# Three shared input buffers, a reordered batch and no closing drain of GpSimd in a gated cross-attention kernel with routed experts

## The chip, the cores and the metric

The kernel runs on one core of a Trainium2 chip. The metric is the device time of one execution in microseconds, lower is better. Engines are named as in the profile: PE (TensorE matmul), PEld (TensorE weight load), DVE (VectorE), ACT (ScalarE), POOL (GpSimd) and SP (SyncE, which here only issues DMAs).

## The reference

x and ctx are (8, 512, 512) float32: 8 batches of 512 rows of width 512. The first layer is a two-way cross-attention between the row-normalised x and ctx, mixed by a gate; the second is a mixture of 8 experts with one expert for each row.

```python
x = x + tanh(g_xattn[0]) * xattn(layernorm(x), ctx)       # see below
x = x + tanh(g_ffn[0])   * ffn(layernorm(x))
# xattn(c, s): c2s = softmax((c Wq_c + b)(s Wk_s + b)^T / sqrt(512)) (s Wv_s + b)
#              s2c = softmax((s Wq_s + b)(c Wk_c + b)^T / sqrt(512)) (c Wv_c + b)
#              gate = sigmoid([c2s, s2c] Wg^T + bg);  gate*c2s + (1-gate)*s2c
# ffn(x): probs = softmax(x router_w + router_b); e = argmax(probs)
#         max(probs) * (x expert_w[e] + expert_b[e])
```

## The kernel before, in words

Every product is made from float32 values split in a high and a low part, in three passes, so one group of 128 rows by 512 columns is 12 matmuls of 128x512 (`product`, L149). The split is made when a PSUM bank is read: ACT copies the high part, then DVE subtracts it (`low`, L1001) and so makes the low part. Only after both is the bank free for its next group.

All engines run the same hand-written list of steps, each engine doing its own share of each step, **in the order of the list**. `opening_steps` (L169) folds weights, `steps_of_a_batch` (L393) is one batch (batch 0 and batch 7 are written out, 1 to 6 are a loop), and `steps_after` (L445) is the tail, where the experts run. The steps that matter here, with direction d (0: x asks ctx, 1: ctx asks x) and tile i of four:

- Q, S, V, U, G: projected queries, scores, values, attended values, gate. On DVE and POOL, G also mixes the two results into `probs` (L1040 to L1049, L1174 to L1181); POOL makes `diff` by three operations a tile.
- PT: transposes of `probs`. M(i): transposes of the previous batch's mixture; MX(i): DVE adds the residual and takes statistics (L1076). NM, NT, LG: normalise, transpose, router logits. RT and RK: routing; in RK POOL scatters token numbers into the lists by four indirect DMAs, waits for them (L1190) and adds 512 to its ids (L1191).
- For the next batch: XS (DVE statistics of an x tile, L1061, then three POOL operations, L1161 to L1163), XN (ACT normalises the tile in place, L937), XD (DVE dot product, L1066), XT (transposes); CD (L1072) and CT for a ctx tile.
- WT: transposes of late weights in batch 0. EX: expert weights in batch 7.

There are two rings of two PSUM banks. "mm" serves Q, V, S and G in turn; "tr" serves PT, CT, XT, M, NT, RK and WT in turn. `take` (L761) makes PE wait, before a group, for the readers of the group two places back in its ring (`wait_readers`, L600): for Q that is `q_lo`, for M(i) it is `x1_done`, which MX(i) sets, for CT `ct_lo`, for S `exp_done`.

x tiles use two buffers and ctx tiles one. SP issues the loads of a batch in a fixed order (`load_next`, `load_rest`, L684 to L693) between the stores of the batch before; each load waits until PE has transposed and DVE has dotted the tile that was in the buffer. So ctx tile t+1 is loaded only after CT and CD of tile t.

Of the kernel before, what the change touches and what calls it, by code (L numbers as in the profile page):

```python
# [32 lines left out]
P = 128  # L33
# [37 lines left out]
def gated_attention_and_experts(nc, x, ctx_in, g_xattn, g_ffn, Wq_c, bq_c, Wk_s, bk_s, Wv_s, bv_s,  # L71
# [10 lines left out]
    with ExitStack() as top:  # L82
        def sb(name, shape, dt=F32):
            return top.enter_context(nc.sbuf_tensor(name, shape, dt))
# [21 lines left out]
        k.x_tile = sb("x_tile", [P, 2, H])  # L106
        k.c_tile = sb("c_tile", [P, H])
# [285 lines left out]
def steps_of_a_batch(first, last):  # L393
# [49 lines left out]

# [22 lines left out]
def attention_part(nc, scope, top, k, x_rows, c_rows, x1_dram, x1_early, list_dram, expert_w,  # L466
# [5 lines left out]
    minus_half, token_ids, x_tile, c_tile = k.minus_half, k.token_ids, k.x_tile, k.c_tile  # L472
    junk, bn_x, mv_x, row_next = k.junk, k.bn_x, k.mv_x, k.row_next
    stage = [x_tile[:, 0], x_tile[:, 1], c_tile[:]]
# [7 lines left out]
    def sem(name):  # L482
        return top.enter_context(nc.semaphore(name))
# [51 lines left out]
    x_loaded = [sem("x_loaded0"), sem("x_loaded1")]  # L535
    c_loaded = sem("c_loaded")
# [5 lines left out]
    waits_passed, waits_passed_dve = sem("waits_passed_by_pool"), sem("waits_passed_by_dve")  # L542

# [82 lines left out]
    def sync(sp, weights_run, experts_run):  # L626
# [57 lines left out]
        def load_next(b):  # L684
            load_c(b, 0)
            load_x(b, 0)
            load_x(b, 1)

        def load_rest(b):
            for t in (1, 2, 3):  # L690
                load_c(b, t)
            load_x(b, 2)
            load_x(b, 3)  # L693
# [4 lines left out]
        load_x(0, 0, first=True)  # L698
        load_weight(0)
        load_weight(1)  # L700
        load_x(0, 1, first=True)
        load_c(0, 0, first=True)
        load_weight(2)
        load_weight(3)
        load_x(0, 2)
        load_x(0, 3)
        load_c(0, 1)
        load_c(0, 2)
# [20 lines left out]
        sp.wait_ge(xt_tr, 4 * B)  # L729
        sp.wait_ge(x_dotted, 4 * B)  # L730
        sp.wait_ge(ct_tr, 4 * B)
        sp.wait_ge(c_dotted, 4 * B)
# [25 lines left out]
    def tensor(pe, weights_run, experts_run):  # L758
# [20 lines left out]
        def run(b, steps):  # L779
            here = turn[0]  # L780
            for step in steps:
# [55 lines left out]
                elif kind == "CT":  # L837
                    pe.wait_ge(c_loaded, 16 * per_batch(bb, i))
                    transposes(bank, lambda n: c_tile[:, tile(n)]).then_inc(ct_tr, 1)
                elif kind == "XT":  # L840
                    pe.wait_ge(x_normed, per_batch(bb, i))
                    transposes(bank, lambda n: x_tile[:, i % 2, tile(n)]).then_inc(xt_tr, 1)
# [45 lines left out]
    def scalar(act, weights_run, experts_run):  # L888
# [3 lines left out]
        def run(b, steps, first=False):  # L892
            for kind, rel, d, i in steps:
# [40 lines left out]
                elif kind == "XN":  # L934
                    act.wait_ge(x_scaled, per_batch(bb, i))
                    rows, stat = x_tile[:, i % 2], mv_x[:, i % 2]
# [43 lines left out]
    def vector(dve, weights_run, experts_run):  # L980
# [25 lines left out]
        def run(b, steps):  # L1006
            for kind, rel, d, i in steps:
# [600 lines left out]
```

## Time and profile before

| what | value |
|---|---|
| median of 3 runs | 1308.49 us (1301.09 to 1313.44) |
| profiled execution, span from first to last instruction | 1297.5 us |
| PE busy | 1201.7 us (93%), 5856 matmuls |
| DVE / ACT / POOL busy | 705.0 (54%) / 416.7 (32%) / 331.2 us (26%) |
| granted TensorE clock, mean | 0.975 |
| HBM read and written | 54.41 and 26.24 MB, 62 GB/s over the span |
| chain that ended last, by engine | PE 52%, POOL 14%, DVE 9%, DMA 9%, issue 7%, ACT 3% |

The profile gives no time of the profiled execution other than its span; the median lies 11.0 us above it, and the fastest run 3.6 us. Shares are of the whole span. Idle time of an engine costs something only if that engine sets the end, and here PE is the one that is nearly always busy. A row of the timeline gives start, duration, engine, line, operation and operands, a count and, in brackets, how long the engine had been idle and what released it.

### The profile page before, as it was taken

The numbers are of one execution on the slowest core, as the hardware profiler recorded it, in microseconds if no ns is written. First come the engines' busy times: TensorE is split into PE (matmuls) and PEld (weight loads), VectorE is DVE, ScalarE is ACT, GpSimd is POOL, SyncE is SP. The second block draws the span as 40 slices with busy tenths as digits, with TensorE's granted clock in tenths as the row PEclk, the third lists the DMA queues.
The fourth block names the chain that finished last, engine by engine and source line by source line (L and its number), as shares of the span: only waits on it lengthen the run. The fifth ranks groups of instructions, "written<-read, shape, count | busy, mean of one in ns | idle before, by whom it ended". The sixth has DMA issues, their size and how long they took to land.

```text
span 1297.5 us, 18153 instructions
## 1 busy us (share of the span) xinstructions
PE 1201.7 (93%) x5856; PEld 978.6 (75%) x5857; DVE 705.0 (54%) x1401; ACT 416.7 (32%) x725; POOL 331.2 (26%) x426
## 2 busy tenths in 40 slices
PE   4999999989998999999999999999999989697995
PEld 3877878867786878787878788878787867576774
DVE  2654656354744474547464746474547446856553
ACT  2333423232233323332333233323332334342331
POOL 1000043103401140214021402240124011655552
PEclk8899999989998999999999999999999999798998
DMA  5131103110212011301120112021302062553541
GB/s 159 34 106 49 57 9 106 17 33 9 80 26 32 24 53 52 33 24 49 57 33 24 51 54 36 21 65 40 33 24 83 23 98 74 169 174 106 147 129 52
DMA packets 61043, 79.39 MB, mean 61 GB/s; under 512 B 28038, under 2 KB 28038, under 8 KB 60872
## 3 DMA queue, kind: packets, MB, share of 16 engines
q1 hardware_dynamic: 48336, 59.94, 18.7%
q0 software_dynamic: 7264, 18.72, 4.6%
q10 hardware_dynamic: 5400, 0.19, 0.3%
q8 instruction: 23, 0.38, 0.1%
q14 instruction: 20, 0.16, 0.0%
HBM read 54.41 MB, written 26.24 MB: 62 GB/s over the span
## 4 chain that ended last, share of the span: by engine, by line
PE 52%; POOL 14%; DVE 9%; DMA 9%; issue 7%; ACT 3%; ACTq 1%; another core or an unknown queue 1%; POOLq 1%; SPq 0%; DVEq 0%
PE mm L156 29%; PE u L819 9%; DMA token_lists<-token_ids,slot_i 7%; PE tr L776 5%; PE e_bank L156 4%; POOL diff L1179 4%; POOL diff L1180 3%; POOL diff L1181 3%; PE w_bank L156 2%; DVE probs L1045 2%; POOL token_lists L1187 2%; DVE q_pair L1004 2%; PE tr L853 1%; DMA x_tile<-in_L_ffn_expert_w 1%
## 5 line engine op out<-in xcount | busy, mean ns | idle before, releaser
L156 PE MATMUL mm<-arena 128*128 128x512 f32 x1536 | 372.3, 394 | 2.7 <-DVE arena L349 1.4
L156 PEld LDWEIGHTS mm<-arena 128*128 128x128 f32 x1536 | 284.2, 188 | 62.3 <-DVE arena L349 1.8
L156 PE MATMUL mm<-arena,q_pair 128*128 128x512 f32 x768 | 196.0, 409 | 12.1 <-ACT probs L909 8.0
L819 PE MATMUL u<-pt_pair,v_pair 128*128 128x512 f32 x768 | 189.7, 397 | 0.0
L156 PEld LDWEIGHTS mm<-arena,q_pair 128*128 128x128 f32 x768 | 145.3, 194 | 48.0 <-ACT probs L909 10.4
L819 PEld LDWEIGHTS u<-pt_pair,v_pair 128*128 128x128 f32 x768 | 139.6, 188 | 28.1 <-DVE pt_pair L1003 1.4
L1003 DVE TENSOR_TENSOR v_pair<-mm,v_pair 128x512 fp32r<-128x512 f32 x64 | 44.3, 692 | 154.2 <-ACT v_pair L904 154.1
L156 PE MATMUL e_bank<-arena,e_pair 128*128 x468 | 121.7, 410 | 1.8 <-issue 0.9
L156 PEld LDWEIGHTS e_bank<-arena,e_pair 128*128 128x128 f32 x468 | 87.4, 193 | 21.5 <-issue 3.1
L156 PE MATMUL mm<-q_pair,arena 128*128 128x512 f32 x384 | 94.1, 394 | 4.7 <-DVE q_pair L1004 4.7
L904 ACT ACTIVATE v_pair<-mm 128x512 fp32r<-128x512 f32 x64 | 38.2, 597 | 179.4 <-PE mm L156 179.4
L1161 POOL TENSOR_SCALAR mv_x<-mv_x 128x1 f32<-128x1 f32 x32 | 7.4, 230 | 342.0 <-DVE mv_x L1062 251.2
L156 PE MATMUL mm<-c2s_pair,arena 128*128 128x512 f32 x384 | 94.4, 395 | 0.0
L156 PEld LDWEIGHTS mm<-q_pair,arena 128*128 128x128 f32 x384 | 71.3, 188 | 23.3 <-DVE q_pair L1004 7.6
L900 ACT ACTIVATE q_pair<-mm,c_col 128x512 fp32r<-128x512 f32 x64 | 44.0, 687 | 137.3 <-PE mm L156 137.3
L1187 POOL DMA_INDIRECT token_lists<-token_ids,slot_i x32 | 31.9, 996 | 211.1 <-DVE slot_i L1120 173.9
L156 PEld LDWEIGHTS mm<-c2s_pair,arena 128*128 128x128 f32 x384 | 71.1, 188 | 14.7
L1004 DVE SCALAR_TENSOR_TENSOR q_pair<-mm,c_col,q_pair 128x512 fp32r<-128x512 f32 x64 | 47.4, 749 | 63.9 <-ACT q_pair L900 62.0
L909 ACT ACTIVATE probs<-mm,neg_top 128x512 f32<-128x512 f32 x64 | 44.0, 687 | 104.5 <-DVE neg_top L1028 104.5
L1179 POOL TENSOR_TENSOR diff<-c2s_pair,q_pair 128x512 f32<-128x512 f32 x32 | 50.5, 1577 | 96.1 <-DVE q_pair L1004 71.2
L776 PE MATMUL tr<-ident,probs 128*128 128x128 f32 x384 | 58.3, 279 | 16.8 <-DVE probs L1049 12.7
L1024 DVE TENSOR_REDUCE mx<-mm 128x1 f32<-128x512 f32 x64 | 44.2, 690 | 46.0 <-PE mm L156 45.0
(157 smaller groups left out, 1544.3 us busy)
## 6 DMA issues: line engine op xcount, KB each, us to landing
x_tile<-in_x SPq DMA_DIRECT2D x64, 256.0 KB, 2.8
c_tile<-in_ctx SPq DMA_DIRECT2D x32, 256.0 KB, 2.7
x_rows<-x_tile SPq DMA_DIRECT2D x32, 256.0 KB
x_rows_early<-x_tile SPq DMA_DIRECT2D x28, 256.0 KB, 2.9
x_tile<-in_L_ffn_expert_w SPq DMA_DIRECT2D x18, 256.0 KB, 2.9
c_tile<-in_L_ffn_expert_w SPq DMA_DIRECT2D x9, 256.0 KB, 2.8
x_tile<-in_L_xattn_Wg SPq DMA_DIRECT2D x8, 256.0 KB, 2.9
e_bias<-in_L_ffn_expert_b SPq DMA_DIRECT2D x1, 1280.0 KB, 7.4
```

Of the source, the lines that this page charges most:

```text
L156: last = pe.matmul(bank, lhsT(a, c), rhs(b, c), start=start and n == 0, stop=stop and n == C * len(PASSES) - 1)
L776: last = pe.transpose(bank[:, tile(n)], block_of(n), ident[:])
L819: last = pe.matmul(u_bank[m][:], v_pair[:, i % 2, a, tile(m)], pt_pair[:, i % 2, p], start=i == 0 and n == 0, stop=i == T - 1 and n == 2)
L900: act.activation(q_pair[:, HI, i], bank[:], ACT.Identity, bias=c_col[:, d, i:i + 1]).then_inc(q_hi, 1)
L909: act.activation(probs[:, i], bank[:], ACT.Exp, bias=neg_top[:, d, i:i + 1], scale=SCALE, accum_out=p_sum[:, d, i:i + 1]).then_inc(exp_don ...
L1003: return dve.tensor_tensor(to, bank, f32(hi), ALU.subtract)
L1004: return dve.scalar_tensor_tensor(to, bank, bias, f32(hi), ALU.add, ALU.subtract)
L1024: then(dve.reduce_max(mx[:, d, i:i + 1], bank[:], axis=AX))
L1179: then(pool.tensor_tensor(diff[:], f32(c2s_pair[:, HI, i]), f32(q_pair[:, HI, i]), ALU.subtract))
L1180: then(pool.tensor_tensor(diff[:], diff[:], f32(c2s_pair[:, LO, i]), ALU.add))
L1181: pool.tensor_tensor(diff[:], diff[:], f32(q_pair[:, LO, i]), ALU.subtract).then_inc(diff_ready, 1)
L1187: pool.indirect_dma_start(out=list_dram, out_offset=bass.IndirectOffsetOnAxis(ap=slot_i[:, t:t + 1], axis=0), in_=token_ids[:, t:t + 1], i ...
```

## The change

1. `x_tile` (2) and `c_tile` (1) become one tensor `in_tile` with three places. Tables say which tile of which kind goes to which place; SP waits by `after_x` and `after_c` for the last user of the place, and loads in a new order. The first two ctx tiles and x tile 0 of a batch are now loaded at the start of the batch before, ahead of `end_batch`.
2. The order of steps changes: M(0), M(1) and MX(0) of the previous batch move from behind Q(0,1) to behind Q(0,2); MX(1), M(2) and NM(0) move from behind Q(0,2) to behind Q(0,3). In the second half of the batch, the preparation of the next batch's tiles is laid out anew.
3. The block is closed with `no_gpsimd_drain=True`.
4. Counting semaphores carry SP's waits, and XS on DVE also waits for XN two tiles back.

```diff
-        k.x_tile = sb("x_tile", [P, 2, H])
-        k.c_tile = sb("c_tile", [P, H])
+        k.in_tile = sb("in_tile", [P, 3, H])
...
-        with nc.Block() as block:
+        with nc.Block(no_gpsimd_drain=True) as block:
...
-    s = cur("Q", 0, 0) + context(2) + cur("Q", 0, 1) + late(0) + context(3) + prev("M", 0) + prev("M", 1) + prev("MX", 0)
-    s += cur("Q", 0, 2) + late(1) + prev("MX", 1) + prev("M", 2) + prev("NM", 0)
-    s += cur("Q", 0, 3) + late(2) + prev("M", 3) + prev("NM", 1)
+    s = cur("Q", 0, 0) + context(2) + cur("Q", 0, 1) + late(0) + context(3)
+    s += cur("Q", 0, 2) + late(1) + prev("M", 0) + prev("M", 1) + prev("MX", 0)
+    s += cur("Q", 0, 3) + late(2) + prev("MX", 1) + prev("M", 2) + prev("NM", 0) + prev("M", 3) + prev("NM", 1)
...
-    s += cur("Q", 1, 0) + late(12) + load(3) + nxt("CD", 0) + cur("Q", 1, 1) + late(13) + load(4) + nxt("XS", 0)
-    s += cur("Q", 1, 2) + late(14) + load(5) + nxt("XS", 1) + cur("Q", 1, 3) + late(15) + nxt("CT", 0) + load(6)
-    s += nxt("XN", 0) + load(7) + cur("S", 1, 0) + nxt("XD", 0) + nxt("XN", 1) + load(8)
-    s += cur("S", 1, 1) + nxt("CD", 1) + nxt("CT", 1) + load(9) + cur("S", 1, 2) + nxt("XD", 1) + load(10)
-    s += cur("S", 1, 3) + load(11) + cur("V", 1, 0) + nxt("CD", 2) + nxt("CT", 2) + cur("PT", 1, 0) + load(12)
-    s += cur("V", 1, 1) + nxt("XT", 0) + cur("PT", 1, 1) + load(13) + cur("U", 1, 0) + table(0)
-    s += cur("V", 1, 2) + nxt("XT", 1) + cur("PT", 1, 2) + load(14) + cur("U", 1, 1) + table(1)
-    s += cur("V", 1, 3) + nxt("CD", 3) + nxt("CT", 3) + cur("PT", 1, 3) + load(15) + cur("U", 1, 2) + load(16) + table(2)
-    s += nxt("XS", 2) + nxt("XN", 2) + nxt("XS", 3) + nxt("XN", 3) + cur("U", 1, 3)
-    s += load(17, 18) + cur("G", 0, 0) + nxt("XD", 2) + nxt("XT", 2) + load(19, 20)
-    s += cur("G", 0, 1) + nxt("XD", 3) + nxt("XT", 3) + load(21, 22)
+    s += cur("Q", 1, 0) + late(12) + load(3) + nxt("CD", 0) + cur("Q", 1, 1) + late(13) + load(4) + nxt("CD", 1)
+    s += cur("Q", 1, 2) + late(14) + load(5) + nxt("XS", 0) + cur("Q", 1, 3) + late(15) + nxt("CT", 0) + load(6)
+    s += nxt("XN", 0) + load(7) + cur("S", 1, 0) + nxt("CT", 1) + load(8)
+    s += cur("S", 1, 1) + nxt("XD", 0) + load(9) + cur("S", 1, 2) + nxt("CD", 2) + load(10)
+    s += cur("S", 1, 3) + load(11) + cur("V", 1, 0) + nxt("CT", 2) + nxt("XT", 0) + cur("PT", 1, 0) + load(12)
+    s += cur("V", 1, 1) + nxt("CD", 3) + nxt("CT", 3) + cur("PT", 1, 1) + load(13) + cur("U", 1, 0) + nxt("XS", 1) + table(0)
+    s += cur("V", 1, 2) + nxt("XN", 1) + cur("PT", 1, 2) + load(14) + cur("U", 1, 1) + nxt("XS", 2) + nxt("XD", 1) + table(1)
+    s += cur("V", 1, 3) + nxt("XN", 2) + nxt("XT", 1) + cur("PT", 1, 3) + load(15) + cur("U", 1, 2) + load(16) + table(2)
+    s += nxt("XS", 3) + nxt("XD", 2) + nxt("XT", 2) + nxt("XN", 3) + cur("U", 1, 3)
+    s += load(17, 18) + cur("G", 0, 0) + nxt("XD", 3) + nxt("XT", 3) + load(19, 20)
+    s += cur("G", 0, 1) + load(21, 22)
...
+IN_PLACES = {("C", 0): (0, 1), ("C", 2): (0, 2), ("X", 2): (0, 3),
+             ("C", 1): (1, 1), ("C", 3): (1, 2), ("X", 3): (1, 3),
+             ("X", 0): (2, 1), ("X", 1): (2, 2)}
...
+        def load_next(b, first=False):
...
+                after_x(b - 1, 2)
             load_c(b, 0)
...
+                after_x(b - 1, 3)
+            load_c(b, 1)
+            after_x(b - 1, 3 if first else 1)
             load_x(b, 0)
...
+        def load_rest(b):
+            after_c(b, 0)
+            load_c(b, 2)
+            after_c(b, 1)
+            load_c(b, 3)
+            after_x(b, 0)
             load_x(b, 1)
+            after_c(b, 2)
             load_x(b, 2)
+            after_c(b, 3)
             load_x(b, 3)
...
             if n == 2:
+                after_c(0, 1)
                 load_c(0, 3)
-                load_next(1)
+                load_next(1, first=True)
...
         with sp.Fori(1, B - 1) as b:
+            load_next(b + 1)
             end_batch(b - 1)
-            load_next(b + 1)
             store_stats(b - 1)
...
                 elif kind == "XS":
-                    dve.wait_ge(x_loaded[i % 2], 16 * per_slot(bb, i))
+                    dve.wait_ge(in_loaded[buf], loads_of("X", bb, i))
+                    if not (isinstance(bb, int) and per_batch(bb, i) <= 2):
+                        dve.wait_ge(x_normed, per_batch(bb, i) - 2)
```

## Rows read from the trace of the kernel before

**Rows 1.** Two batches: stretch, length, busy time by engine, clock, DMA

```profile
204.05:338.86 134.81, 128.44 (x622) 105.18 (x623) 70.61 (x147) 40.70 (x73) 31.06 (x41) 0.97 0.16 40
732.57:860.13 127.56, 125.64 (x622) 103.36 (x623) 70.50 (x147) 40.71 (x73) 31.12 (x41) 1.00 0.18 41
```

**Rows 2.** Waits of PE: waiter, releaser, total us, times, longest

```profile
PE tr L776 <- DVE probs L1049: 12.7, 8, 5.8
...
PE tr L776 <- DMA c_tile<-in_ctx: 9.2, 6, 1.9
```

**Rows 3.** Timeline of batch 1 around CT(1) and S(1,2)

```profile
271.30 0.24 POOL L1191 TENSOR_SCALAR token_ids<-token_ids 128x4 int32<-128x4 int32 x1 [14.57 <-DMA token_lists<-token_ids,slot_i]
271.33 0.66 PE L776 MATMUL tr<-ident,c_tile 128*128 128x128 f32 x4 [1.90 <-DMA c_tile<-in_ctx]
...
273.12 0.81 ACT L937 ACTIVATE x_tile<-x_tile,mv_x 128x512 f32<-128x512 f32 x1 [8.51 <-POOL mv_x L1163]
...
274.65 3.78 PE L156 MATMUL mm<-arena,q_pair 128*128 128x512 f32 x8 [2.66 <-ACT probs L909]
```

**Rows 4.** Timeline of batch 5, the same place

```profile
795.17 0.23 POOL L1191 TENSOR_SCALAR token_ids<-token_ids 128x4 int32<-128x4 int32 x1 [10.17 <-DMA token_lists<-token_ids,slot_i]
...
797.68 0.67 ACT L909 ACTIVATE probs<-mm,neg_top 128x512 f32<-128x512 f32 x1
...
798.49 2.63 PEld L156 LDWEIGHTS mm<-arena,q_pair 128*128 128x128 f32 x12 [0.33 <-ACT probs L909]
...
798.60 0.69 DVE L1024 TENSOR_REDUCE mx<-mm 128x1 f32<-128x512 f32 x1
...
799.72 0.69 ACT L909 ACTIVATE probs<-mm,neg_top 128x512 f32<-128x512 f32 x1 [0.17 <-DVE neg_top L1028]
...
800.39 0.59 ACT L928 ACTIVATE arena<-tr 128x512 fp32r<-128x512 f32 x1
```

**Rows 5.** Timeline, end of batch 1: U(1,3), G, then M(0) and M(1)

```profile
308.12 0.82 ACT L937 ACTIVATE x_tile<-x_tile,mv_x 128x512 f32<-128x512 f32 x1 [4.34 <-POOL mv_x L1163]
...
309.65 0.81 ACT L937 ACTIVATE x_tile<-x_tile,mv_x 128x512 f32<-128x512 f32 x1 [0.71 <-POOL mv_x L1163]
310.37 2.40 ACT L918 ACTIVATE q_pair<-u,bv_col 128x512 fp32r<-128x512 f32 x4
...
311.96 3.05 PE L156 MATMUL mm<-q_pair,arena 128*128 128x512 f32 x12 [0.61 <-DVE q_pair L1004]
...
338.02 0.69 DVE L1049 TENSOR_TENSOR probs<-probs,q_pair 128x512 f32<-128x512 f32 x1
338.63 1.40 DVE L1004 SCALAR_TENSOR_TENSOR q_pair<-mm,c_col,q_pair 128x512 fp32r<-128x512 f32 x2
...
338.86 1.06 PE L776 MATMUL tr<-ident,probs 128*128 128x128 f32 x8 [0.99 <-DVE probs L1049]
```

**Rows 6.** Timeline, end of Q(0,3) of batch 2, and MX(1)

```profile
344.12 0.74 DVE L1081 SCALAR_TENSOR_TENSOR x_tile<-tr,tanh_g,x_tile 128x512 f32<-128x512 f32 x1
...
345.49 0.58 PEld L776 LDWEIGHTS tr<-ident,probs 128*128 128x128 f32 x4
...
345.92 0.69 ACT L900 ACTIVATE q_pair<-mm,c_col 128x512 fp32r<-128x512 f32 x1 [1.50 <-PE mm L156]
...
346.64 0.75 DVE L1004 SCALAR_TENSOR_TENSOR q_pair<-mm,c_col,q_pair 128x512 fp32r<-128x512 f32 x1 [0.71 <-ACT q_pair L900]
```

**Rows 7.** Timeline, transposes right behind V(1,1), and DVE's part

```profile
289.07 0.58 PEld L776 LDWEIGHTS tr<-ident,x_tile 128*128 128x128 f32 x4
...
290.73 0.68 DVE L1003 TENSOR_TENSOR arena<-tr,arena 128x512 fp32r<-128x512 f32 x1
```

**Rows 8.** Timeline of PE in batch 0: CT(3), and WT(8)

```profile
74.93 0.63 PE L776 MATMUL tr<-ident,c_tile 128*128 128x128 f32 x4 [1.47 <-DMA c_tile<-in_ctx]
...
106.59 0.66 PE L776 MATMUL tr<-ident,x_tile 128*128 128x128 f32 x4 [0.98 <-DVE pt_pair L1003]
```

**Rows 9.** Instructions of the block's end: durations in ns, start

```profile
L127 POOLq DRAIN  x1: 9059/9059/9059, 1288.2 to 1288.2; - x1
```

More of the change, by code:

```diff
@@ L471, in attention_part @@
     rank_of_e, list_end = k.rank_of_e, k.list_end
-    minus_half, token_ids, x_tile, c_tile = k.minus_half, k.token_ids, k.x_tile, k.c_tile
+    minus_half, token_ids, in_tile = k.minus_half, k.token_ids, k.in_tile
     junk, bn_x, mv_x, row_next = k.junk, k.bn_x, k.mv_x, k.row_next
-    stage = [x_tile[:, 0], x_tile[:, 1], c_tile[:]]
+    stage = [in_tile[:, i] for i in range(3)]
     def sb(name, shape, dt=F32):
@@ L534, in attention_part @@
     ids_ready, listed = sem("ids_ready"), sem("listed")
-    x_loaded = [sem("x_loaded0"), sem("x_loaded1")]
-    c_loaded = sem("c_loaded")
+    in_loaded = [sem(f"in_loaded{i}") for i in range(3)]
     res_loaded = [sem("res_loaded0"), sem("res_loaded1")]
@@ L554, in tile, with place_of, loads_of @@
         return slice(i * P, (i + 1) * P)
+    def place_of(kind, b, t):
+        places = IN_PLACES_FIRST if isinstance(b, int) and b == 0 else IN_PLACES
+        return places[kind, t][0]
+    def loads_of(kind, b, t):
+        places = IN_PLACES_FIRST if isinstance(b, int) and b == 0 else IN_PLACES
+        buf, nth = places[kind, t]
+        return 16 * (IN_LOADS[buf] * b + nth)
     def keys_of(d):
@@ L682, in load_expert @@
             sp.dma_start(stage[place], expert_w[e, tile(c), :]).then_inc(ex_loaded[place], 16)
-        def load_next(b):
-            load_c(b, 0)
-            load_x(b, 0)
+        def load_next(b, first=False):
+            if first:
+                after_c(b - 1, 2)
+            else:
+                after_x(b - 1, 2)
+            load_c(b, 0)
+            if first:
+                after_c(b - 1, 3)
+            else:
+                after_x(b - 1, 3)
+            load_c(b, 1)
+            after_x(b - 1, 3 if first else 1)
+            load_x(b, 0)
+        def load_rest(b):
[4 more added lines that the diff above has]
+            after_x(b, 0)
             load_x(b, 1)
-        def load_rest(b):
-            for t in (1, 2, 3):
-                load_c(b, t)
+            after_c(b, 2)
             load_x(b, 2)
+            after_c(b, 3)
             load_x(b, 3)
@@ L697, in sync @@
         sp.sem_inc(stats_copied, 16)
-        load_x(0, 0, first=True)
+        load_x(0, 0)
         load_weight(0)
         load_weight(1)
-        load_x(0, 1, first=True)
-        load_c(0, 0, first=True)
+        load_x(0, 1)
+        load_x(0, 2)
         load_weight(2)
         load_weight(3)
-        load_x(0, 2)
+        after_x(0, 0)
         load_x(0, 3)
+        after_x(0, 1)
+        load_c(0, 0)
+        after_x(0, 2)
         load_c(0, 1)
+        after_c(0, 0)
         load_c(0, 2)
@@ L727, in sync @@
             load_rest(b + 1)
[L729 to L732, printed above, removed]
+        after_x(B - 1, 3)
+        after_c(B - 1, 3)
         for n in range(3):
@@ L837, in run @@
                 elif kind == "CT":
-                    pe.wait_ge(c_loaded, 16 * per_batch(bb, i))
-                    transposes(bank, lambda n: c_tile[:, tile(n)]).then_inc(ct_tr, 1)
+                    buf = place_of("C", bb, i)
+                    pe.wait_ge(in_loaded[buf], loads_of("C", bb, i))
+                    transposes(bank, lambda n: in_tile[:, buf, tile(n)]).then_inc(ct_tr, 1)
                 elif kind == "XT":
                     pe.wait_ge(x_normed, per_batch(bb, i))
-                    transposes(bank, lambda n: x_tile[:, i % 2, tile(n)]).then_inc(xt_tr, 1)
+                    buf = place_of("X", bb, i)
+                    transposes(bank, lambda n: in_tile[:, buf, tile(n)]).then_inc(xt_tr, 1)
                 elif kind == "M":
@@ L935, in run @@
                     act.wait_ge(x_scaled, per_batch(bb, i))
-                    rows, stat = x_tile[:, i % 2], mv_x[:, i % 2]
+                    rows, stat = in_tile[:, place_of("X", bb, i)], mv_x[:, i % 2]
                     act.activation(rows, rows, ACT.Identity, bias=stat[:, 1:2],
@@ L1065, in run @@
                     dve.wait_ge(x_normed, per_batch(bb, i))
-                    dve.tensor_tensor_reduce(out=junk[:], in0=x_tile[:, i % 2], in1=u_row[:, 0], scale=SCALE,
+                    dve.tensor_tensor_reduce(out=junk[:], in0=in_tile[:, place_of("X", bb, i)], in1=u_row[:, 0], scale=SCALE,
                                              scalar=u_const[:, 0:1], op0=ALU.mult, op1=ALU.add,
@@ L1070, in run @@
                 elif kind == "CD":
-                    dve.wait_ge(c_loaded, 16 * per_batch(bb, i))
-                    dve.tensor_tensor_reduce(out=junk[:], in0=c_tile[:], in1=u_row[:, 1], scale=SCALE,
+                    buf = place_of("C", bb, i)
+                    dve.wait_ge(in_loaded[buf], loads_of("C", bb, i))
+                    dve.tensor_tensor_reduce(out=junk[:], in0=in_tile[:, buf], in1=u_row[:, 1], scale=SCALE,
                                              scalar=u_const[:, 1:2], op0=ALU.mult, op1=ALU.add,
```

36 lines of the change are left out of this document (22 added, 14 removed).

## The prediction, made before the result was known

> **What bounds the kernel now.** I read the busy shares first: PE works in 93% of the 1297.5 us span, so a change gains or loses only what it does to PE's idle time, to the TensorE clock, or to the end behind the last matmul. Next the busy time in stretches, cut where M(0) starts [rows 1]: a batch takes 127.6 us at best and 134.8 us at worst, with the same number of matmuls. Then PE's waits [rows 2] and the timeline at each. One batch has four places where PE idles, of which three matter here:
>
> - **Place A**, S(1,2). CT(1) waits 1.90 us for its ctx tile, then S(1,2) waits 2.66 us more for the exp of S(1,0) [rows 3]. The ctx wait looks like what three shared buffers would cure. But behind S(1,0) stands another chain: POOL waits for its token scatter (released at 271.30), then runs XS(0), which lets ACT run XN(0) at 273.12, and only behind XN(0) comes the exp. S(1,2) starts 3.35 us after POOL's release in batch 1 (274.65 - 271.30), and 3.32 us after it in batch 5 (798.49 - 795.17), where no ctx tile is waited for at all [rows 3, 4]. So the scatter pins S(1,2), with or without the ctx wait.
> - **Place B**, G(0,0)'s second half: 0.61 us, because ACT does XN(2) and XN(3) (308.12, 309.65) before it reads U's banks at 310.37 [rows 5].
> - **Place C**, M(0): 0.99 us until the last mixture is made [rows 5], in each of 7 transitions between batches; the 5.8 us among the 12.7 is in the tail, which keeps its order [rows 2].
>
> **The change, part by part**, against the profiled execution (span 1297.5 us).
>
> Ctx and x loads earlier. In batch 0, CT(3)'s wait of 1.47 us [rows 8] goes: no scatter stands behind it. In batches 1 to 6 the ctx wait goes and place A's wait takes its place in full, since RK, XS(0), XN(0), S(1,0) keep their order on POOL and ACT: 0. Sum **-1.5**. SP's stores, residual loads and stat stores keep their order; the early loads pass them only in a stretch in which their places have long been free. The load of ctx tile 3 now falls beside the scatter; its cover is the scatter's own wait, and bounds are given below.
>
> Place B. XS(3), XN(3) take the place of XS(2), XN(2), so ACT is free one XN step earlier: 309.65 - 308.12 = 1.53 us. U(1,3) ends 0.43 us later for PE, because XT(2) now precedes it, and is still read in time; the wait of 0.61 us goes, and POOL's mixing chain starts 1.53 us earlier.
>
> Place C. The mixture is then ready at 338.71 - 1.53 = 337.18. But moving M(0) and M(1) behind Q(0,2) uncovers another wait: Q(0,2) takes Q(0,0)'s bank, and DVE makes that bank's low part only after the last mixture. It starts at 338.63 for two in 1.40 us, so one is 0.70, ready at 337.18 - 0.08 + 0.70 = 337.8 [rows 5]. PE comes there at 338.86 - 0.99 - 0.61 = 337.26, and waits until 337.9. Before, PE was through the two sets of transposes (0.87 us) and started Q(0,2) at 339.7; the same work is now done by 337.9 + 0.87 = 338.8. Gain 0.9 a transition, 6.3 for seven, and 0.3 more in batch 0, where place B's wait is nearly 1 us: **-6.6**. I count nothing for less contention between POOL and XD(2).
>
> **M(3), a new wait.** M(3) takes M(1)'s bank, so PE waits for MX(1). MX(1) stood behind Q(0,2) and now stands behind Q(0,3) on DVE, which must first make that group's low part. With PE through Q(0,3) at 345.49 [rows 6]: ACT at 345.92, DVE from 346.64 for 0.75 to 347.39, then MX(1) for 0.74 (as at 344.12) to 348.13, which is 2.64 us. M(2) fills 0.43 of them. PE idles 2.2 us, seven times: **+15.5**. Nothing is between to cover it; S(0,0) is next in PE's queue. Bounds: 1.5 (DVE hands over with overlap) and 2.7.
>
> **PT(1,0), a new wait.** CT(2), XT(0), PT(1,0) are now three tr groups in a row, and PT(1,0) needs CT(2)'s bank. Behind V, transposes that start at 289.07 have their low part made at 290.73 + 0.68 = 291.41, 2.34 us later [rows 7], because ACT and DVE read V's bank first. Two sets of transposes cover 0.87: idle 1.47 us in batches 0 to 6, **+10.3**. The trace has such a triple once, in batch 0 (PT(0,1), WT(7), WT(8)): 0.98 us [rows 8], the lower bound, as no V bank comes first there.
>
> S(1,3), a new wait. On DVE, CT(1)'s low part now stands ahead of S(1,1)'s maximum, and its high part must come first, behind the exp on ACT. The exp is at 797.68 [rows 4], copy 0.67 later (as 799.72 to 800.39) for 0.59, low part 0.69 to 799.6 instead of the maximum's start at 798.60. The exp of S(1,1) goes from 799.72 to 800.7, and its bank is free 0.81 later (as 797.68 to 798.49) at 801.5, while S(1,2) ends at 798.49 + 2.75 = 801.24. About 0.4 us, six times: **+2.4**; bounds 0 and 0.6.
>
> The closing drain. It holds POOL for 9.06 us, 1288.2 to 1297.3, and the span ends with it [rows 9]. All stores have been waited for before, so **-9.1**; bounds -9.1 and 0 (if the same time is paid after the last instruction, which the span can't show). The first is nearer to the row, and I take it.
>
> The Trainium skill (Runtime: NRT & Kernel Launch, "The ~15µs preamble/postamble breakdown") puts a barrier that waits for all engines behind the kernel; by that rule whatever POOL still has to finish would be waited for there, and the sum would be +20.1 instead of +11.0. No row here shows what follows the span.
>
> Semaphore increments on SP and the added DVE wait for XN two tiles back: 0, these have passed long before; without that cover one wait would cost under 0.1 us.
>
> Sum: -1.5 - 6.6 + 15.5 + 10.3 + 2.4 - 9.1 = **+11.0 us**, a span of 1308.5. The shown median is 11.0 above the span; I add the sum to it: **1320 us**.
>
> **Bounds of what rows don't show.** The scatter with ctx tile 3 loaded beside it: the releases come 14.57 and 10.17 us after the wait began in batches 1 and 5 [rows 3, 4], so 4.4 us is the spread between batches, and I take from -1 to +1 us in each of 6. The clock: batch 1 exceeds batch 5 by 7.25 us, of which waits explain 4.6; 2.6 us is at a lower granted clock (0.97 against 1.00) [rows 1]. One new wait of 2.2 us might do the same in some batches: 0 to +9 in all. Together with the bounds above, the forecast's own case spans 1307 to 1332.
>
> **The rivals.**
> 1. **The drain's time is paid anyway.** Everything else as forecast: 1319.5 + 9.1 = 1329, slower by 1.6%. It decides as soon as more than 2.1 us of the 9.1 come back behind the span. For it: the drain took long although all DMAs had landed, so POOL has some work of its own there. Against: nothing after it needs POOL's results. 26%.
> 2. **The new waits are not there.** If DVE makes MX(1) and CT(2)'s low part in time, M(3), PT(1,0), S(1,3) cost 0: 1308.5 - 1.5 - 6.6 - 9.1 = 1291, faster by 1.3%. For it: DVE is 54% busy only. Against: the 0.98 us [rows 8] is just such a wait. 16%.
> 3. **The scatter is quicker**, as in batch 5, in all batches, because fewer loads lie beside it: 4 to 7 us less in batches 1 and 2, about 20 in all. With the new waits 1300, without them 1271. Against: the residual loads stay where they were. 8%.
> 4. The change hides its loads and nothing else moves, since order and drain cancel out: 1307. 8%.
>
> **How the numbers follow.** My forecast has 42%. A measurement of this kernel can hardly tell less than 1% (13 us) from no change. The forecast's 1320 lies 0.9% above, so I part its 42% into 24 same and 18 slower. Rival 1 gives 23 slower, 3 same; rival 2 gives 13 faster, 3 same; rival 3 gives 5 faster, 3 same; rival 4 same. Faster 0.18, same 0.41, slower 0.41. The range 1291 to 1332 leaves out rival 3's fast end and the upper end of rival 1.
>
> **What would show it.** Right: a wait of about 2.2 us of PE for L1081 (MX) in each batch at M(3), one of about 1.5 us for L1003 at PT(1,0), S(1,2) still 3.3 us behind POOL's L1191, no wait for a ctx tile, no wait of M(0) for L1049 but a short one of Q(0,2) for L1004, and a span that ends about 1 us after the last store has landed. Wrong: PE's idle time in a batch below 5 us, a scatter whose wait changes by over 3 us, or a median over the span by 20 instead of 11 us.

## The result, and the profile after

| | before | after |
|---|---|---|
| median, same chip | 1308.49 us (1301.09 to 1313.44, 5 runs) | 1318.45 us (1316.46 to 1319.86, 5 runs) |
| ratio, 95% interval | | 1.0082 [1.0052, 1.0112] |
| span of the profiled execution | 1297.5 us | 1317.2 us (its own time 1318.96 us) |

The kernel became 10.0 us slower; +11.0 was forecast. Ratios leave out three single executions of the experiments that lay far above the rest (1366.65, 1453.64 and 2409.02 us). The two spans differ by 19.7 us, so the two profiled executions are not equally typical, and that must be settled first. The page of after, its busy shares:

```profile
span 1317.2 us, 18354 instructions
PE 1205.0 (91%) x5856; PEld 985.2 (75%) x5857; DVE 698.8 (53%) x1401; ACT 416.9 (32%) x725; POOL 335.6 (25%) x426
```

PE's work did not grow, but its idle time did. The stretches of batches 1, 2 and 5, columns as in [rows 1], now cut where Q(0,2) starts, which stands ahead of M(0):

```profile
202.08:338.21 136.13, 127.26 (x622) 104.53 (x622) 69.84 (x147) 40.72 (x73) 31.54 (x41) 0.99 0.18 40
338.21:480.43 142.22, 128.23 (x622) 105.24 (x622) 69.79 (x147) 40.73 (x73) 31.59 (x41) 0.96 0.21 37
753.71:885.47 131.76, 125.99 (x622) 103.40 (x622) 69.78 (x147) 40.73 (x73) 31.60 (x41) 1.00 0.17 40
```

Batch 5 takes 4.2 us more than in [rows 1]. Batch 2 is the longest at 142.22 us. PE's waits, which answer to [rows 2], say why:

```profile
PE mm L155 <- ACT probs L952: 29.7, 6, 9.9
...
PE mm L155 <- DVE q_pair L1047: 13.3, 8, 6.6
PE tr L817 <- DVE x_tile L1128: 12.6, 7, 1.9
PE tr L817 <- DVE arena L1046: 8.0, 7, 1.1
PE tr L817 <- DVE probs L1092: 5.8, 1, 5.8
...
PE tr L817 <- DMA x_tile<-in_L_xattn_Wv_s: 1.0, 1, 1.0
```

The ctx tile is gone from the list, and M(0)'s wait for the mixture (L1092, was L1049) is left only in the tail (5.8). New are seven waits for `x_tile` (M(3)), seven for `arena` (PT(1,0)) and, under `q_pair`, seven of 0.97 us (Q(0,2)), beside one of 6.6 us in batch 7, where before has three of together 5.3 (1.31, 1.75 and 2.26). The 29.7 us for `probs` are S(1,2), place A. One of them is 9.9 us, in batch 2. Its timeline, answering to [rows 3, 4]:

```profile
412.67 0.23 POOL L1238 TENSOR_SCALAR token_ids<-token_ids 128x4 int32<-128x4 int32 x1 [19.95 <-DMA token_lists<-token_ids,slot_i]
414.47 0.81 ACT L980 ACTIVATE in_tile<-in_tile,mv_x 128x512 f32<-128x512 f32 x1 [13.60 <-POOL mv_x L1210]
415.19 0.67 ACT L952 ACTIVATE probs<-mm,neg_top 128x512 f32<-128x512 f32 x1
...
416.00 3.35 PE L155 MATMUL mm<-arena,q_pair 128*128 128x512 f32 x7 [9.88 <-ACT probs L952]
```

POOL is released at 412.67 and S(1,2) starts at 416.00, 3.33 us later, where [rows 3, 4] had 3.35 and 3.32. The chain is untouched; its head, the scatter, was late. The row also shows what such a stall does to the clock: PE idles from 406.1, the granted clock is 0.59 in the stretch from 410 to 416 us and 0.56 in that from 416 to 422, and 1.00 again behind it. That is near the lower of the clock's two levels (1.2 of 2.4 GHz), and the first seven matmuls of S(1,2) take 3.35 us, where twelve of Q(0,2) below take 3.04.

A second profile of the same kernel (below) shows 16.4 us in place of 29.7. The profiled execution of after took 1318.96 us, 0.5 above its median, so it is typical in time: its loop is long, and its stretch from M(0) of batch 7 to the end is short (293.5 us, 304.0 in the second profile). That of before has no time of its own, but its span is 11.0 us below the median, and time and span are 1.7 to 1.9 us apart in every execution on record: it was about 9 us short. The medians are the comparison.

The transition into batch 2, answering to [rows 5, 6]:

```profile
337.41 1.40 DVE L1047 SCALAR_TENSOR_TENSOR q_pair<-mm,c_col,q_pair 128x512 fp32r<-128x512 f32 x2
...
338.21 3.04 PE L155 MATMUL mm<-arena 128*128 128x512 f32 x12 [0.98 <-DVE q_pair L1047]
...
344.49 0.59 PEld L817 LDWEIGHTS tr<-ident,probs 128*128 128x128 f32 x4
...
344.91 0.69 ACT L943 ACTIVATE q_pair<-mm,c_col 128x512 fp32r<-128x512 f32 x1 [2.94 <-PE mm L155]
...
345.63 0.75 DVE L1047 SCALAR_TENSOR_TENSOR q_pair<-mm,c_col,q_pair 128x512 fp32r<-128x512 f32 x1 [0.99 <-ACT q_pair L943]
...
346.30 0.74 DVE L1128 SCALAR_TENSOR_TENSOR x_tile<-tr,tanh_g,x_tile 128x512 f32<-128x512 f32 x1
...
347.10 0.42 PEld L817 LDWEIGHTS tr<-ident,probs 128*128 128x128 f32 x4 [2.02 <-DVE x_tile L1128]
347.10 0.66 PE L817 MATMUL tr<-ident,probs 128*128 128x128 f32 x4 [1.79 <-DVE x_tile L1128]
```

Read it from below. M(3) starts at 347.10, when MX(1) on DVE (L1128) ends. MX(1) starts behind the low part of Q(0,3) (L1047), which follows ACT's copy. The first matmul row shows Q(0,2) waiting 0.98 us for the low part that queues behind the last mixture. PT(1,0) in the same batch, answering to [rows 7]:

```profile
426.65 1.03 PEld L817 LDWEIGHTS tr<-ident,in_tile 128*128 128x128 f32 x8
...
427.70 0.69 DVE L1046 TENSOR_TENSOR v_pair<-mm,v_pair 128x512 fp32r<-128x512 f32 x1 [0.70 <-ACT v_pair L947]
...
428.31 1.28 DVE L1046 TENSOR_TENSOR arena<-tr,arena 128x512 fp32r<-128x512 f32 x2
429.04 0.42 PEld L817 LDWEIGHTS tr<-ident,probs 128*128 128x128 f32 x4 [1.37 <-DVE arena L1046]
429.05 0.66 PE L817 MATMUL tr<-ident,probs 128*128 128x128 f32 x4 [1.14 <-DVE arena L1046]
```

CT(2) and XT(0) are the eight transposes at 426.65; DVE makes V's low part first, then CT(2)'s, and only then may PT(1,0) start. Batch 0, answering to the first row of [rows 8]:

```profile
79.59 0.63 PE L817 MATMUL tr<-ident,x_tile 128*128 128x128 f32 x4 [1.03 <-DMA x_tile<-in_L_xattn_Wv_s]
```

CT(3) no longer waits, but a late weight tile does, whose load now stands behind early tile loads in SP's queue. The block's end, answering to [rows 9]:

```profile
L126 POOLq EVENT_SEMAPHORE  x2: 17/17/17, 1317.0 to 1317.1; - x2
```

The drain is gone, and the last store's issue (1314.52, 0.98 us long) is followed by the end after 1.7 us.

### The profile page after: what moved, and what is told of

Same layout as the page of the kernel before. It is cut to its first block, busy times and chain, and to the rows that moved or that the text cites. A ratio compares the mean times of both kernels' runs of the same rounds, so it can differ in the third digit from the quotient of the medians.

```text
span 1317.2 us, 18354 instructions
## 1 busy us (share of the span) xinstructions
PE 1205.0 (91%) x5856; PEld 985.2 (75%) x5857; DVE 698.8 (53%) x1401; ACT 416.9 (32%) x725; POOL 335.6 (25%) x426
## 4 chain that ended last, share of the span: by engine, by line
PE 54%; POOL 14%; DMA 10%; DVE 10%; issue 5%; ACT 4%; ACTq 1%; POOLq 1%; DVEq 0%; SPq 0%
PE mm L155 29%; PE u L860 9%; DMA token_lists<-token_ids,slot_i 8%; PE e_bank L155 6%; PE tr L817 5%; POOL diff L1226 4%; POOL diff L1227 3%; POOL diff L1228 3%; DVE q_pair L1047 2%; PE w_bank L155 2%; DVE probs L1088 2%; POOL token_lists L1234 2%; DMA in_tile<-in_L_ffn_expert_w 1%; PE tr L896 1%; PE e_bank L1601 1%
## 5 line engine op out<-in xcount | busy, mean ns | idle before, releaser
L155 PE MATMUL mm<-arena 128*128 128x512 f32 x1536 | 374.5, 396 | 14.7 <-DVE q_pair L1047 13.3
L155 PE MATMUL mm<-arena,q_pair 128*128 128x512 f32 x768 | 200.3, 415 | 29.7 <-ACT probs L952 29.7
L155 PEld LDWEIGHTS e_bank<-arena,e_pair 128*128 128x128 f32 x468 | 87.1, 193 | 19.5 <-issue 1.3
L1208 POOL TENSOR_SCALAR mv_x<-mv_x 128x1 f32<-128x1 f32 x32 | 13.7, 428 | 339.0 <-DVE mv_x L1108 248.0
L1047 DVE SCALAR_TENSOR_TENSOR q_pair<-mm,c_col,q_pair 128x512 fp32r<-128x512 f32 x64 | 47.4, 749 | 78.1 <-ACT q_pair L943 78.1
L817 PE MATMUL tr<-ident,probs 128*128 128x128 f32 x384 | 58.8, 280 | 30.5 <-DVE x_tile L1128 12.6
L1046 DVE TENSOR_TENSOR arena<-tr,arena 128x512 fp32r<-128x512 f32 x80 | 54.3, 688 | 60.2 <-ACT arena L971 49.5
L817 PEld LDWEIGHTS tr<-ident,probs 128*128 128x128 f32 x384 | 45.8, 142 | 43.1 <-DVE x_tile L1128 14.3
```

What stands on the lines that cost most here:

```text
L155: last = pe.matmul(bank, lhsT(a, c), rhs(b, c), start=start and n == 0, stop=stop and n == C * len(PASSES) - 1)
L817: last = pe.transpose(bank[:, tile(n)], block_of(n), ident[:])
L1046: return dve.tensor_tensor(to, bank, f32(hi), ALU.subtract)
L1047: return dve.scalar_tensor_tensor(to, bank, bias, f32(hi), ALU.add, ALU.subtract)
```

## The experiments

Ratios are to the kernel before on the same chip. Its medians were 1293.51, 1298.6 and 1296.47 us in the three series, so only ratios are compared across series.

### The control: the kernel after, again

> The changed kernel once more, as the control for the runs beside it on this chip. Theory A (the order of steps, not the chip, makes it slower): again 0.5 to 1.1% above the kernel before, with 1.79 us of PE at M(3), 0.97 at Q(0,2), 1.14 at PT(1,0) in each batch, to the hundredth as in the first trace; only the wait of S(1,2), which hangs on the scatter, differs from run to run (29.7 us in the first trace, 17.7 to 19.9 in three runs of its variants).

Measured: 1317.54 us, 1.0133 [1.0092, 1.0173], span 1310.7. The stretch of batch 2, and the waits of PE for ACT and for the two new places:

```profile
337.68:475.70 138.02, 127.28 (x623) 104.55 (x623) 69.78 (x147) 40.72 (x73) 31.60 (x41) 0.98 0.20 38
```

```profile
PE mm L155 <- ACT probs L952: 16.4, 6, 6.6
...
PE tr L817 <- DVE x_tile L1128: 12.6, 7, 1.9
PE tr L817 <- DVE arena L1046: 8.0, 7, 1.1
```

The waits of DVE's making are the same to 0.1 us; the scatter's went from 29.7 to 16.4. The former belong to the order, the latter varies from run to run. The intervals of the two comparisons (1.0052 to 1.0112, 1.0092 to 1.0173) overlap only from 1.0092 to 1.0112, so the ratio of after is known to half a per cent. I use the middle of the two, 1.0108, below.

### The drain, alone, from both sides

After with the drain:

```
-    with nc.Block(no_gpsimd_drain=True) as block:
+    with nc.Block() as block:
```

> The changed kernel with the closing drain of GpSimd put back, nothing else. Theory A (the drain's 9.06 us are real time at the end): span and median rise by about 9 us over the changed kernel's 1318.45, to about 1327, ratio to the kernel before 1.015. Theory B (the same time is paid after the last instruction when the drain is gone): the span rises by 9, the median stays at 1318, and the time outside of the span falls.

Measured: 1315.59 us, 1.0153 [1.0126, 1.018], span 1314.9, profiled execution 1316.68. Before without the drain, the reverse edit:

> The kernel before without the closing drain, nothing else. Theory A: 9 us less than the kernel before, about 1299, ratio 0.993. Theory B: no difference, 1308. The two profiled executions also show how far the kernel before moves from run to run by itself.

Measured: 1287.45 us, 0.9951 [0.9934, 0.9968], span 1286.0, profiled execution 1287.73. The block's end in after with the drain, then in before without it:

```profile
L126 POOLq DRAIN  x1: 9059/9059/9059, 1305.7 to 1305.7; - x1
```

```profile
L127 POOLq EVENT_SEMAPHORE  x2: 17/17/17, 1285.8 to 1285.9; - x2
```

The time outside the span is 1.8 us with the drain and 1.7 without. Over all runs of all kernels it is 1.7 to 1.9 us. So nothing of the 9.06 us is paid afterwards: rival 1 falls. The gain by medians is 6.1 us on before (4 to 8.5 by the interval of the ratio), and by ratios 2.6 to 9 us on after (1.0153 against 1.0133 and 1.0082, which were measured on other chips). A third pair, below, gives 8.5.

After itself was not run on the chip of this series. After with the drain less the drain (9.06 us, or the 6.1 of before) puts it at 1.0083 to 1.0106 there. The next two edits of after, M in its old place and CT(2) one step earlier, ran on this chip, so this is the value to hold them against.

### M in its old place

```
-    s = cur("Q", 0, 0) + context(2) + cur("Q", 0, 1) + late(0) + context(3)
-    s += cur("Q", 0, 2) + late(1) + prev("M", 0) + prev("M", 1) + prev("MX", 0)
-    s += cur("Q", 0, 3) + late(2) + prev("MX", 1) + prev("M", 2) + prev("NM", 0) + prev("M", 3) + prev("NM", 1)
+    s = cur("Q", 0, 0) + context(2) + cur("Q", 0, 1) + late(0) + context(3) + prev("M", 0) + prev("M", 1) + prev("MX", 0)
+    s += cur("Q", 0, 2) + late(1) + prev("MX", 1) + prev("M", 2) + prev("NM", 0)
+    s += cur("Q", 0, 3) + late(2) + prev("M", 3) + prev("NM", 1)
```

> The changed kernel with M, MX and NM of the previous batch in their old places behind Q(0,1), Q(0,2) and Q(0,3). Theory A (moving MX(1) behind Q(0,3) made PE wait at M(3), and moving M uncovered Q(0,2)'s bank): the 7 waits of 1.8 us for DVE x_tile and the 7 of 0.97 us of Q(0,2) for DVE q_pair go, about 19 us, and M(0) waits under 0.2 us, since place B's gain stays: 1299. Theory B (M is late whatever its place, the wait only changes its name): M(0) waits 1 us and more in each batch, 1311 or above.

Measured: 1287.38 us, 0.9941 [0.9922, 0.9961], span 1290.7. PE's waits:

```profile
PE mm L155 <- ACT probs L952: 19.9, 6, 5.8
...
PE tr L817 <- DVE probs L1092: 8.4, 8, 5.8
PE tr L817 <- DVE arena L1046: 8.0, 7, 1.1
PE mm L155 <- DVE q_pair L1047: 7.5, 1, 7.5
```

`x_tile` has left the list, `q_pair` is down to one, and M(0) waits 8.4 - 5.8 = 2.6 us in seven transitions, 0.37 each, instead of 0.99 before. By the idle column that is 1.79 + 0.98 - 0.37 = 2.4 us a transition, 16.8 in seven; start to start (M(3) starts 2.61 us after M(2), and 0.44 of it is M(2)'s own) M(3)'s wait is 2.17 and the sum 19.5. Measured: 0.9941 against 1.0108, 21.6 us (against 1.0082 or 1.0083, 18). A third measure is the length of batch 5, where the clock is 1.00 in every profile, less its wait of S(1,2): 130.12 us in the control and 127.47 here (128.91 - 1.44), 2.65 us a batch or 18.6 in seven. **The moved M steps are the largest loss of the change.** M(0) was expected to wait under 0.2 us and waits 0.37. The shared buffers and the new order of the tile preparation, which were left in, are worth 0.99 + 0.61 - 0.37 = 1.2 us a transition together; no run separates the two.

### MX(1) ahead of Q(0,3)

```
-    s += cur("Q", 0, 2) + late(1) + prev("M", 0) + prev("M", 1) + prev("MX", 0)
-    s += cur("Q", 0, 3) + late(2) + prev("MX", 1) + prev("M", 2) + prev("NM", 0) + prev("M", 3) + prev("NM", 1)
+    s += cur("Q", 0, 2) + late(1) + prev("M", 0) + prev("M", 1) + prev("MX", 0) + prev("MX", 1)
+    s += cur("Q", 0, 3) + late(2) + prev("M", 2) + prev("NM", 0) + prev("M", 3) + prev("NM", 1)
```

> The changed kernel with MX(1) alone moved ahead of Q(0,3), M in the new places. Theory A (M(3) waits because DVE makes Q(0,3)'s low part before MX(1)): the 7 waits of 1.79 us for DVE x_tile go, the 7 of 0.97 us of Q(0,2) for DVE q_pair stay: 12.5 us below the changed kernel, ratio to the kernel before about 1.002. Theory B (DVE is late there anyway, and MX(1) ahead only makes Q(0,3)'s low part late for S(0,0)): a wait of 1 us or more for DVE q_pair at S(0,0), ratio 1.007 or above.

Measured: 1303.62 us, 1.004 [1.0011, 1.0069], span 1307.7. PE's waits:

```profile
PE mm L155 <- ACT probs L952: 19.3, 6, 4.4
...
PE tr L817 <- DVE x_tile L1128: 1.6, 6, 0.3
```

The wait at M(3) falls from 12.6 to 1.6 us and nothing else appears in the loop. The time falls by 0.68% from the middle of the two comparisons of after, 9 us (5 and 12 from the two by themselves, on other chips), where 11.0 went from the list. Batch 5 less its wait of S(1,2) goes from 130.12 to 128.54 us, 1.58 a batch. DVE's order behind M(1), and not DVE's speed, made this wait.

### CT(2) one step earlier

```
-    ... cur("S", 1, 2) + nxt("CD", 2) + load(10)
-    ... cur("V", 1, 0) + nxt("CT", 2) + nxt("XT", 0) + cur("PT", 1, 0) + load(12)
+    ... cur("S", 1, 2) + nxt("CD", 2) + nxt("CT", 2) + load(10)
+    ... cur("V", 1, 0) + nxt("XT", 0) + cur("PT", 1, 0) + load(12)
```

> The changed kernel with CT(2) moved from behind V(1,0) to behind S(1,2), so that no three groups of the tr ring stand in a row ahead of PT(1,0). Theory A (PT(1,0) waits for CT(2)'s bank): the 7 waits of 1.14 us for DVE arena go and nothing takes their place, 8 us, 1310. Theory B (PT(1,0) is held by the last normalised row of probabilities, which is ready at about the same time): the waits stay with DVE probs as releaser, 1318.

Measured: 1297.54 us, 1.0019 [1.0001, 1.0037], span 1296.3. PE's waits:

```profile
PE mm L155 <- ACT probs L952: 17.7, 6, 5.3
...
PE tr L817 <- DVE x_tile L1128: 12.6, 7, 1.9
```

The seven waits for `arena` are gone, and no other came. They were 8.0 us in the list (10.6 start to start), and the time fell by 8 to 11.5 us (from 1.0082 or 1.0108). Batch 5 less its wait of S(1,2) goes from 130.12 to 128.54 us (129.15 - 0.61), 1.58 a batch, 11.1 in seven. The triple in the tr ring is the second loss.

### The scatter's wait taken off place A

POOL waits for its scatter only behind U(1,3), in the kernel after and in the kernel before:

```
                         in_=token_ids[:, t:t + 1], in_offset=None).then_inc(listed, 16)
+                    if not in_tail[0]:
+                        continue
                     await_count(pool, waits_passed, listed, 16 * T * (bb + 1))
...
+                elif kind == "U" and d == 1 and i == T - 1 and not first:
+                    await_count(pool, waits_passed, listed, 16 * T * b)
+                    pool.tensor_scalar(token_ids[:], token_ids[:], float(L), None, ALU.add).then_inc(ids_ready, 1)
```

> The changed kernel, but POOL waits for its token scatter (and adds 512 to its ids) only at the end of the batch, behind U(1,3), and not ahead of XS(0). Order of all other steps as in the changed kernel. Theory A (S(1,2) is pinned by POOL's wait for the scatter, through XS(0) and XN(0)): PE's waits for ACT probs, about 19 us in batches 1 to 6, go, and up to 5 us at the lower clock: 20 us below the changed kernel, ratio to the kernel before 0.99 to 0.995. Theory B (S(1,2) is late for DVE's and ACT's own work, as CT(1) now stands ahead of S(1,1) there): most of the wait stays, 0 to 5 us.

Measured on after: 1290.16 us, 0.9925 [0.9894, 0.9956], span 1287.7. The control ran on the same chip: 27 us less than its 1317.54, where 20 were expected.

> The kernel before with the same edit. Theory A: the exp of S(1,0) is on time, but CT(1) still waits for its ctx tile, which is loaded only behind CT(0) in the single buffer: PE's waits for ACT probs (8 to 10 us) go, those for the ctx tile (7 to 9 us) stay or grow, 10 us below the kernel before, ratio 0.992. So the shared buffers would be worth their 8 us only once the scatter's wait is out of the way. Theory B (the scatter pins nothing in the kernel before, the ctx tile alone does): no difference, 1.00.

Measured on before: 1278.54 us, 0.9852 [0.9806, 0.9897], span 1288.5, where 0.992 was expected. Its six executions fall in two groups, four from 1278.1 to 1278.9 us and two at 1290.3 and 1290.5, and the profile is of one of the latter. PE's waits in after with the late wait, then in before with it:

```profile
PE mm L155 <- DVE q_pair L1047: 13.9, 8, 7.2
...
PE tr L817 <- DVE x_tile L1128: 12.6, 7, 1.9
PE tr L817 <- DVE arena L1046: 8.0, 7, 1.1
```

```profile
PE tr L776 <- DVE probs L1049: 12.6, 8, 5.8
PE mm L156 <- DVE q_pair L1004: 11.0, 8, 6.4
PE tr L776 <- DMA c_tile<-in_ctx: 7.7, 6, 2.0
```

In neither is there a wait of S(1,2) for the exp (`probs` of ACT). In before the ctx waits stay, 7.7 us (9.2 without the edit). So before had two limits in parallel at place A. The scatter was the later one, and the ctx wait costs something only once the scatter is out of the way. That is what my zero for place A said, and it is now shown from both sides. A batch without a ctx wait, in before with the late wait:

```profile
719.29:846.56 127.27, 125.48 (x623) 103.24 (x623) 70.52 (x147) 40.59 (x73) 30.74 (x41) 1.00 0.17 41
```

The same batch in after with the late wait:

```profile
720.73:850.37 129.64, 125.54 (x622) 103.53 (x622) 69.84 (x147) 40.84 (x73) 31.52 (x41) 1.00 0.15 41
```

Both run at a clock of 1.00. **The new order costs 2.37 us a batch** where neither scatter nor ctx is waited for. The idle column says 1.79 (M(3)) + 1.14 (PT(1,0)) + 0.98 (Q(0,2)) - 0.99 - 0.61 (M(0) and G before) = 2.31.

On before the late wait brought 19 us, but the waits for ACT that it removes are 8.0 us in before's profile:

```profile
PE mm L156 <- ACT probs L909: 8.0, 5, 2.7
```

Batch 1 of before with the late wait shows most of the rest, beside the first of [rows 1]:

```profile
202.78:331.05 128.27, 125.59 (x623) 103.25 (x623) 70.49 (x147) 40.57 (x73) 30.78 (x41) 1.00 0.17 42
```

The clock is 1.00 instead of 0.97, and PE does the same matmuls in 125.59 instead of 128.44 us. From M(0) of batch 1 to M(0) of batch 7 before takes 787.6 us and the version with the late wait 771.9. Of these 15.7 us, 8.0 are the waits for ACT, 1.6 are ctx waits, and 6.0 are PE's busy time (760.9 to 755.0). The same stretch of the control takes 801.1 us, and 777.8 with the late wait: 16.4 us of waits and 6.9 of PE's busy time. **The stalls at place A cost 6 to 7 us of clock on top of the waiting.** The profile's span is only 9.0 us shorter than before's, because outside this stretch it is 6.7 us longer. What sets the two groups of executions 12 us apart stays open, and so do the 3 to 4 us that are left of the gain.

### All three together

After with M in its old place, CT(2) earlier and the late wait, run under two names, and the same with the drain:

> The changed kernel with three edits together: M, MX and NM in their old places, CT(2) behind S(1,2), and POOL's late wait for the scatter. Theory A (the four waits are separate and add up): -18 for M, -8 for CT(2), -20 for the scatter: some 46 us below the changed kernel, ratio to the kernel before 0.972, PE idle under 1 us in a batch of the loop. Theory B (one wait gone uncovers another, as M's move did): gains overlap, ratio 0.98 or above, with a new releaser in the list of PE's waits.

> The version with the three edits once more, beside the next run: 0.966 to 0.973 of the kernel before.

> The version with the three edits and the closing drain of GpSimd. Its loop hardly depends on the scatter, so its runs should scatter less (within 4 us) than those of the kernel before and the drain's price can be read better than from the first pair (6 us by medians, 9.06 in the profile). Theory A: 9 us above the same version without the drain. Theory B (part of the drain's time is other waiting at the end that stays): 6 us.

Measured: 1259.88 us, 0.9694 [0.9658, 0.9729]; again 1261.55 us, 0.9726 [0.9695, 0.9756]; with the drain 1270.05 us, 0.9793 [0.9764, 0.9822], that is 8.5 us more than again. Against the control on the same chip the first is 57.7 us faster, where 46 were expected; the three edits alone gave 18 to 22, 8 to 11.5 and 20 to 27 us, so they add up and none hides another. Two batches of the first, and PE's waits in it:

```profile
326.13:451.75 125.62, 125.01 (x622) 103.47 (x623) 69.75 (x147) 40.73 (x74) 31.49 (x41) 1.00 0.22 42
702.99:828.61 125.62, 125.00 (x623) 103.49 (x623) 69.74 (x147) 40.75 (x74) 31.52 (x41) 1.00 0.17 42
```

```profile
PE e_bank L1607 <- ACT e_normed L1457: 15.9, 10, 5.2
...
PE tr L817 <- DVE probs L1092: 8.5, 8, 5.8
PE mm L155 <- DVE q_pair L1047: 5.6, 1, 5.6
```

Batches 2 and 5 are alike to 0.01 us at a clock of 1.00, and PE is busy in 125.0 of 125.62 us. This version is about 3% faster than before and 4% faster than after. But for M(0)'s 0.4 us, what is left to wait for lies in the opening, the last batch and the tail.

## Why the prediction was right

The forecast was +11.0 us by my first mechanism, and +10.0 was measured. The mechanism is shown term by term, but that the two numbers lie within 1 us is in part luck: several terms were off and partly cancel, and the interval is 6.8 to 14.7. Point by point:

- **Place A at zero: right.** S(1,2) of batch 2 kept its 3.33 us behind POOL's release (3.35 in batch 1), no ctx wait was left, and the late wait showed both sides. But its size moves: ctx and exp waits in the loop together are 15.7 and 15.1 us in the profiles of before with and without the drain, and 29.7, 16.4 and 18.5 in those of after, again and with the drain.
- **M(3), +15.5: right in mechanism, a little large.** The wait is for MX(1), 2.17 us start to start against the forecast 2.2 (15.2 in seven), but 1.79 in the idle column, and taking all but 0.27 of it away shortened a batch by 1.58.
- **PT(1,0), +10.3: right.** 429.04 - 426.65 = 2.39, less 0.87 for the two sets, is 1.52 us against 1.47 (10.6 in seven), 1.14 in the idle column. Moving CT(2) took it away and shortened a batch by 1.58.
- **Q(0,2) and places B, C, -6.6: right in mechanism, too large by the idle column.** The mixture was ready 0.3 us later than I had it (the last operation starts at 336.80 and takes 0.69), and Q(0,2) waited 0.98 instead of about 0.6. So 0.99 + 0.61 - 0.98 = 0.62 us a transition, 4.3 in all. I had booked the gain to the move of M as well; it is the buffers and the new order of the tile preparation that bring it (1.2 a transition), and the move takes half of it away.
- **S(1,3), +2.4: right in kind, too large.** My own figures give 801.5 - 801.24, 0.3 us and not 0.4. The idle column shows no wait of 0.3 us or more there, but from the start of S(1,2) to that of V(1,0) it is 5.92 us in batch 5 of after and 5.70 in batch 5 of before: 0.2 us a batch, 1.3 in six, hidden in PE's busy time.
- **CT(3) in batch 0, -1.5: wrong, -0.4.** Its wait went, but the load of WT's tile then came 1.0 us late. I had said that the early loads pass nothing that matters in SP's queue. I had looked at stores and residual loads, not at batch 0's weights.
- **The drain, -9.1: right in place.** Three pairs give 6.1, 8.5 and, on after, 2.6 to 9 us; the rows show 9.059 each time. Why the pairs by medians fall short was not settled.
- **The median above the span: my reading was wrong, and harmless.** I added the sum to a median 11.0 above the span. The gap between time and span is 1.7 to 1.9 us, and the rest was the spread of executions. Said as "a median over the span by 20" my own test of rival 1 would have misled me had the profile after been a short execution. The Trainium skill (Runtime: NRT & Kernel Launch, "The ~15µs preamble/postamble breakdown") has a barrier for all engines behind the kernel; the runs show no more than these 1.9 us outside the span, with or without the drain, so the measurement decides.

The sum with terms taken start to start is -0.4 - 4.3 + 15.2 + 10.6 + 1.3 - 9.1 = +13.3; with the idle column for the waits (12.6 and 8.0, nothing at S(1,3)) +6.8. The batches themselves decide between the two. Batch 5 without its wait of S(1,2) takes 127.56 us in before and 130.10 to 130.12 in the three profiles of the new order with that wait, all at a clock of 1.00. That is +2.56 a batch, where my terms make 3.2, and 7 x 2.56 - 0.4 - 9.1 = +8.4. The measured 10.0 lies 1.6 above, well inside its interval, and the control's 17 [12, 22] lies 9 above; no profile of before from that chip is on record that could say where.

The rivals: the drain's time is not paid anyway (1). The new waits are there (2). The scatter is not quicker (3):

| us from first scatter issue to release, batch | 1 | 2 | 3 | 4 | 5 | 6 | 7 | tail |
|---|---|---|---|---|---|---|---|---|
| before | 19.6 | 19.75 | 17.75 | 16.89 | 15.07 | 17.53 | 18.29 | 11.66 |
| after | 19.58 | 24.85 | 20.23 | 19.03 | 16.63 | 19.02 | 20.43 | 12.99 |
| after, again | 18.31 | 21.61 | 17.01 | 17.17 | 15.11 | 16.84 | | |

Summed over batches 1 to 6, before has 106.6 and before without the drain 106.0. The kernels of the new order give 119.3 (after), 106.1 (again), 108.2, 109.6, 107.4 and 108.9. Without the profile of after, an outlier, the new order's mean is 108.0, some 2 us above before, within my -6 to +6 and within the spread of the kernels; that the ctx load beside the scatter makes the difference is not shown. One of my signs of being wrong, a scatter whose wait changes by over 3 us, did show in the profile of after (24.85 against 19.75 us in batch 2). The second profile has 21.61 there, so the sign was set inside what one kernel does by itself. Rival 4 (order and drain cancel, 1307) falls too: the order costs about twice what the drain gives back.

My bound for the clock, 0 to +9 us, held: PE's busy time in the loop is 760.9 us in before, 764.5 in after and 760.0 in the control. In these three profiles the batches that wait over 3 us at place A have a granted clock of 0.96 to 0.99 (9.88 us of waiting and 0.96 in batch 2 of after), and those that wait up to 2 us have 1.00. The new waits at M(3), PT(1,0) and Q(0,2) cost no clock: with the late wait after has them all and 1.00 in every batch of the loop.

## What to carry to other kernels

A wait at the head of an engine's list hides the wait behind it: before crediting a load that comes earlier, follow the other chains into the same instruction, and find which ends last in a batch where the first wait is absent. Where PSUM banks are shared in a ring, moving a group for PE also moves it in the readers' queues; a group that follows the two before it in a ring of two with no other work of PE between cost 1 to 2 us each time here, and each such wait could be removed by moving one step. A blocking wait for DMAs in an in-order queue belongs where its result is used, not where it was issued: here that alone was worth as much as anything in the change.

## What was not expected of the hardware

- GpSimd's closing drain takes 9.059 us in the profile of each of four kernels, to the nanosecond, though all stores had been waited for, and it is real time of the program: the medians of two pairs differ by 6.1 and 8.5 us.
- Four indirect scatters of 128 elements of 4 bytes each take 15 to 25 us until their semaphore while tiles are being loaded, 11.5 to 13.0 us in the tail. They differ by 3 us between two executions of the same kernel in the same batch (24.85 against 21.61 us in batch 2 of after). Why was not tried.
- A short stall costs clock as well as time. Behind 9.88 us of waiting the granted clock was 0.56 for the next 6 us, and the stalls at place A cost 6.0 us of PE's busy time in the loop of before and 6.9 in that of the control. The shorter waits of after, up to 1.9 us each, left the clock at 1.00.
